# Skewed bands of a windowed attention: where the two half transfers stand

## The reference

```
xn  = layernorm(x)
disp, val = (xn @ W_disp), (xn @ W_val)            # per head: 16 and 8 wide
strain[t, j] = disp[t - 63 + j] - disp[t]          # j = 0..63
logit[t, j]  = gelu(strain @ W_strain + rel[j] @ W_pos) @ W_bond
               - 10 * sigmoid(gelu(strain @ W_dmg + b_dmg) @ W_dmg_out + b_dmg_out)
w   = softmax over j (positions before the start masked)
out[t] = sum_j w[t, j] * val[t - 63 + j]
x  += out @ W_cproj + experts(xn)
```

## Time and profile before

| | |
|---|---|
| median of 3 runs | 1132.99 us (1130.6 to 1134.23) |
| the profiled execution | 1132.02 us |
| its span in the profile | 1130.3 us |
| PE busy | 972.2 us (86%) |
| DVE busy | 908.1 us (80%) |
| ACT busy | 788.0 us (70%) |
| band reads | 8 of 2048 KB |
| band writes | 16 of 512 KB |
| zero fills of the bands | 8 of 1024 KB |

### The profile page before, as it was taken

One profiled execution on the slowest core, in us unless ns is written; L12 is line 12 of the kernel. 1 busy time (PEld: TensorE's weight loads), 2 busy tenths in 40 slices (PEclk: granted clock), 3 DMA queues, 4 the chain that ended last, 5 costly groups with the idle time before them and its releaser, 6 DMA issues. The chain is left out here.

```text
span 1130.3 us, 23604 instructions
## 1 busy us (share of the span) xinstructions
PE 972.2 (86%) x9302; PEld 518.5 (46%) x9302; DVE 908.1 (80%) x1006; ACT 788.0 (70%) x859; POOL 532.7 (47%) x549
## 2 busy tenths in 40 slices
PE   6687777889788899999998579998999999989897
PEld 4422222333466344433343578534646465555533
DVE  7987888899776999999997777677686667476856
ACT  3689999999764799999998642431366656555573
POOL 6088888528506558888887204407710000000172
PEclk9899999999988899999999789997799999999999
DMA  9891000012187222222211684000314335432121
GB/s 312 226 367 36 31 34 33 24 40 67 46 266 216 75 61 70 74 75 75 75 53 38 187 296 139 1 0 26 97 57 122 99 116 140 122 103 85 38 59 45
DMA packets 102212, 113.75 MB, mean 101 GB/s; under 512 B 11509, under 2 KB 86737, under 8 KB 98385
## 3 DMA queue, kind: packets, MB, share of 16 engines
q1 hardware_dynamic: 93876, 98.15, 28.6%
q0 software_dynamic: 6656, 13.91, 3.6%
q10 hardware_dynamic: 1571, 0.20, 0.1%
HBM read 66.48 MB, written 42.59 MB: 96 GB/s over the span
## 5 line engine op out<-in xcount | busy, mean ns | idle before, releaser
L260 DVE SCALAR_TENSOR_TENSOR ring<-AD,PT 128x1808 f32<-128x1808 f32 (+15 forms) x128 | 282.2, 2221 | 28.6 <-PE LG L983 26.8
L983 PE MATMUL LG<-ring,lred 128*32 128x456 f32 (+15 forms) x2048 | 235.3, 579 | 0.0
L266 POOL DMA_INDIRECT ys<-rows,goali x80 | 160.5, 2006 | 81.8 <-DVE rows L867 49.4
L2336 DVE TENSOR_REDUCE MX<-SS 128x2 f32<-128x1024 f32 x119 | 144.5, 1218 | 55.6 <-PE SS L2053 55.5
L2266 ACT ACTIVATE EX<-SS 128x1024 f32<-128x1024 f32 x128 | 130.3, 1031 | 77.6 <-PE SS L2053 77.1
L923 ACT ACTIVATE ring<-ring 128x3680 f32<-128x3680 f32 (+15 forms) x47 | 161.1, 3429 | 3.6 <-DVE ring L260 3.6
L1008 PE MATMUL SD<-DSf,eyes 99*32 99x456 bf16 (+15 forms) x1280 | 97.1, 380 | 69.4 <-ACT ring L928 64.7
L929 ACT ACTIVATE ring<-ring 128x1824 f32<-128x1824 f32 (+15 forms) x80 | 145.7, 1822 | 0.0
L776 POOL DMA_INDIRECT xs<-rows,sloti x64 | 123.9, 1935 | 29.6 <-issue 19.2
L1970 POOL DMA_INDIRECT XN<-ys,sloti x16 | 16.3, 1017 | 246.7 <-PE SS L2063 242.2
L260 DVE SCALAR_TENSOR_TENSOR ring<-AD,bdmg 128x1808 f32<-128x1808 f32 (+15 forms) x48 | 106.4, 2216 | 0.0
(11 more groups left out here) (430 smaller groups left out, 1689.5 us busy)
## 6 DMA issues: line engine op xcount, KB each, us to landing
ring<-band SPq DMA_DIRECT2D x6, 2048.0 KB, 12.2
w1s<-in_L_ffn_W SPq DMA_DIRECT2D x39, 256.0 KB, 2.9
w2s<-in_L_ffn_W SPq DMA_DIRECT2D x39, 256.0 KB, 2.9
band<-Z SPq DMA_DIRECT2D x8, 1024.0 KB
xl<-xs SPq DMA_DIRECT2D x20, 272.0 KB, 2.9
xs<-Z SPq DMA_DIRECT2D x5, 1024.0 KB, 9.9
w1s<-w1d SPq DMA_DIRECT2D x80, 64.0 KB
w2s<-w2d SPq DMA_DIRECT2D x80, 64.0 KB
```

The costliest lines, as they stand in the source:

```text
L260: return v.scalar_tensor_tensor(out=tile[:, s, :, t0:T], in0=AD[:, s, :, j + t0:j + T], scalar=extra, in1=AD[:, s, :, PAD + t0:PAD + T], o ...
L266: pool.indirect_dma_start(ys0[:, :], bass.IndirectOffsetOnAxis(ap=goali[:, 4 * n + a:4 * n + a + 1], axis=0), yo[:, n % 2, a, :], None, bo ...
L983: mm = pe.matmul(LG[32 * b:32 * b + 32, par, s, t0:T], lred[:, s, n % 4, :], ring[:, slot, s, b, t0:T], start=(n % 4 == 0), stop=(n % 4 == 3))
L2336: v.tensor_reduce(MX[:, t, p // 2, hh:hh + 2], pairs_of(b, name), AX.X, ALU.max).then_inc(freed[slot], 1)
```

## The change

The row shift moves from the write to the read. A tile is written by one transfer of 128 rows to columns 0 to 2047 of `band[k]`, unshifted; only the right half of each row need be zero, so the fill at the start is four transfers of 1 MB in place of eight. The read is two transfers of 64 partitions; its rows are 16 KB long but start 32 columns short of a row apart, so that row `i` begins `32 * i` columns before its own data, in the zeros of the row above. The counts of the semaphores `written`, `landed` and `d_zero` follow. SP's order becomes write(0), read(0), write(1), write(2), read(1), write(3), read(2), read(3), and its wait for `landed(0)` goes.

```diff
                     for par in range(NT):
-                        for half in range(2):
-                            sp.dma_start(band[par][:, 32 * WIN * half:32 * WIN * half + 32 * WIN], zeros.rearrange("p q t -> p (q t)")
-                                         ).then_inc(d_zero, 16)
+                        sp.dma_start(band[par][:, 32 * WIN:], zeros.rearrange("p q t -> p (q t)")).then_inc(d_zero, 16)
...
-                        act.wait_ge(d_zero, 192)
+                        act.wait_ge(d_zero, 128)
...
             def written(k):
-                return d_out[k], 32 * (g + 1)
+                return d_out[k], 16 * (g + 1)
 
             def landed(k):
-                return d_in[k], 16 * (g + 1)
+                return d_in[k], 32 * (g + 1)
...
                 sp.wait_ge(*written(k))
-                sp.dma_start(wide[k % WIDE].rearrange("r s n -> r (s n)"), band[k]).then_inc(landed(k)[0], 16)
+                for r0 in range(0, P, 64):
+                    rows = dram_rows(band, (k * P + r0) * 32 * P, [[32 * P - 32, 64], [1, 32 * P]])
+                    sp.dma_start(wide[k % WIDE][r0:r0 + 64].rearrange("r s n -> r (s n)"), rows).then_inc(landed(k)[0], 16)
...
                     sp.wait_ge(ex_ready, 5 * g + k + 2)
-                    for r0 in range(0, P, 64):
-                        rows = dram_rows(band, (k * P + r0) * 32 * P, [[32 * P + 32, 64], [1, 32 * WIN]])
-                        sp.dma_start(rows, zs[k][r0:r0 + 64].rearrange("p s n -> p (s n)")).then_inc(written(k)[0], 16)
+                    sp.dma_start(band[k][:, 0:32 * WIN], zs[k].rearrange("p s n -> p (s n)")).then_inc(written(k)[0], 16)
...
                 if g == 0:
-                    sp.wait_ge(d_zero, 192)
+                    sp.wait_ge(d_zero, 128)
                 write(0)
                 read(sp, 0)
                 write(1)
+                write(2)
                 read(sp, 1)
-                sp.wait_ge(*landed(0))
-                write(2)
                 write(3)
                 for k in range(2, NT):
                     read(sp, k)
```

## The result

The changed kernel takes 1148.01 us (median of 4 runs, 1143.46 to 1149.42) against 1132.32 before (4 runs): 1.0151 times as long, interval 1.0115 to 1.0188. The profiled execution, the longest of its four runs, has a span of 1147.5 us against 1130.3, +17.2; between the medians it is +15.7.

A forecast was written before the change was run, and what follows sets the result against it. PE is busiest, so time moves only where it waits for band transfers in the two combine stages: +2.0 and +1.0 us make +3.0 on 1132.0, 1135.0, or 1136.0 on the runs' scale; range 1125 to 1141.

The forecast's parts named there:

- Softened half rate: Both combine stages: a half read's data take 9.2 us behind other work, 9.8 on an empty queue; chance 0.46.
- the 280: Band reads in both stages: reads above 280 GB/s would show the forecast wrong; 200 to 230 would show it right.
- The transfers into DSf: 32-row SBUF-to-SBUF transfers at 198 GB/s, share 1.03, taken as evidence that writing into part of the partitions is slow.
- The start and end of a read: First stage, read(0): of 8.6 us only the 7.1 of data was replaced, by 9.8, giving +2.7 us.
- Write(0): First stage: as one transfer, 4.4 us from its issue to the read behind it instead of 6.9, -2.5 us.
- Write(2) ahead of read(1): First stage: read(1) stands behind a further 1.05 MB, partly covered by its own start, +1.6 us.
- Turn(1): First stage: starts 3.4 us later, after 4.0 us idle instead of 0.6, and falls to the lower clock, +2.2 us.
- Turn(2) in the first stage: No wait for its read but a 2.6 us stop for ACT; ends at 360.5 against 358.5, stage +2.0 us.
- ACT's tail: First stage: ACT's casts and side copy after turn(1) end at 356.1 instead of 350.47, delaying its turn(2) copies.
- The second stage: Second combine stage at the same prices: turn(3) starts at about 690 instead of 688.98, +1.0 us.
- slow rival: Both stages: queued half reads also take 10.4 us; first stage +3.8, second +5.4, time 1142; chance 0.36.
- The zero fills: Start of kernel: dropping half the fills, some 10 us of DMA, costed at nothing; without cover a gain up to 10 us.

## Why the prediction was wrong

- *The mechanism and its sign were right.* A row of a half read takes about twice as long (1.28 us for 0.61), the read pays more than the write gains, and the wait passes on from turn to turn.
- *The step that failed is "Softened half rate": 9.2 us for a half read behind other work, 9.8 on an empty queue.* Measured 10.7 (read(1)) and 10.55 (read(0)). I let one row, write(1) in halves at 313 GB/s, pull the price down from the 10.4 that write(0) gave. A queue full of work doesn't soften a half read: in their windows the reads of the first stage ran at 225, 203 and 211 GB/s (the last, read(2), from 345.2 to 354.2), none near the 280 that I had named as the sign of it. The transfers into DSf that I took as a second slow row were no clean witness: in that stretch all their packets are under 2 KB, so they differ from the fills in more than the partitions.
- *The start and end of a read were taken as unchanged.* The 7.1 us for the data of a whole read were about right (7.3), and I kept 1.5 us around them. In halves read(0) has 2.5: its first row starts 1.30 us after the issue (0.97 before), and turn(0) 1.17 us after the end of the last row (0.44 before). The cut reads of the kernel before show the same, 1.27 and 1.09. So read(0) costs 4.3 us more where I took +2.7; about 0.5 of the miss lies in its data and 1.1 in start and end. At read(1) the data alone miss 1.5 us (10.7 for 9.2). Why the end grows, no run shows.
- *Write(0)* was nearly right: 3.95 us, predicted 4.4.
- *Write(2) ahead of read(1), +1.6,* was wrong: the order alone gave 8.6 us for that read and no change of the time. I had let only the read's own start cover the write, but SP also waits for write(1) to land before it issues read(1). In the kernel before with the new order write(1) moves its last row until 326.04 and read(1) its first from 328.16; most of write(2), 325.75 to 329.21, falls in between (row times from the trace).
- *Turn(1)* starts 4.9 us later relative to the stage's start (342.21 - 335.12 - 2.15), predicted 3.4, after 2.93 us idle, predicted 4.0. Its clock fell, as said, but not for the whole of it: granted 0.69 from 342.2 to 347.7, a mean between the two levels of 1.2 and 2.4 GHz. That turn(0) would stand 5.37 us and run at 0.54, I had not put down.
- *Turn(2) in the first stage* was to wait for ACT; it waited 2.83 us for its read. ACT's tail was nearly as late (its side copy ends at 358.16), so the stage came out at 362.12, +1.4 relative, against my +2.0. The further 3.3 us of that stage come behind turn(2): a stop of 2.24 us in turn(3) that waits for nothing the profile shows, and behind it 128 gather matmuls that took 3.82 us in place of 1.99; a last wait of 1.39 us where 3.29 stood gives 1.9 back. I did not predict this stop. Smaller ones stand in the kernel before too (0.75 us at 338.27, 1.05 at 665.94). All three end 1.2 to 1.6 us after the end of a 16 KB packet of an instruction queue (q8 in the DMA view; here from 371.05 to 372.69), and so do the like stops in the middle of a turn or a gather of the other kernels. That points to code that came late, but no run moved these packets, and the cause is not shown.
- *The second stage* was to cost +1.0. The price comes at each of its reads: relative to the stage's start, turn(1) is 4.5 us late, turn(2) 4.8, and turn(3), which had no wait, stands 3.59 us and is 7.6 late; it runs at the lower clock as well, to 709.49. In all +9.0. My slow rival had this chain, with turn(3) 5.4 late, and ended at 1142: the right case, too cheap. Of what it fell short, 4.5 us lie in the two stages of the profiled execution (13.7 against 9.2); the rest lies outside them.
- *The zero fills* at nothing: right as far as the time can tell.

## What to carry over

When the row count of a transfer changes, look at which partitions it reaches before counting bytes: here the half reads, and half writes on an empty queue, moved some 200 to 230 GB/s, band transfers over both sides 260 to 420. If one side of a round trip through DRAM has to be cut that way, cut the smaller one: here the write of 1 MB (about 9 us a kernel) and not the read of 2 MB (26 us). And where two rows disagree on a price, a slow one on the empty queue and a fast one in a crowd, forecast with the slow one unless the fast one has the same form and the same size.

## What the runs showed of the hardware

- Two halves issued 0.01 us apart on two queues were not interleaved: all 16 engines took one queue's 1 MB (242 GB/s), then the other's (227). A second queue did not make two slow halves into one fast transfer, and it put a write ahead of a read that was wanted first (10.8 us to land).
- A half write behind a whole read overlaps its partner (313 GB/s in the earlier trace rows, 0.31 us a row of 8 KB); so does one behind a read in halves (write(1) of the kernel with cut reads: 3.5 us for its 1 MB, 0.31 us a row). A half read behind two plain writes does not (203). Cutting the reads in half again, sides in turn, gave 213. What lets the one overlap and not the other was not settled.
- The first stage began between 299.3 and 301.9 us in the profiled executions, with eight fills from 299.3 to 301.4 and with four from 300.2 to 301.9. The ranges overlap, so a difference of 2 us ahead of a stage in two single profiles is not yet an effect of a change.
